# Reordering three queues of a mixture-of-experts stage: later weight pieces behind the tokens' rest, a norm's variance product behind the up products, the last norm's scaling last

## The reference, cut to what matters

```python
x = _layernorm(x + _L0_ffn_ref(x, gate_weight, gate_up_weights, down_weights, shared_gate_up, shared_down))
# in _L0_ffn_ref: 8 routed experts (F = 352), the best two for each token, and one shared expert (Fs = 704)
gu = einsum('th,efh->tef', x, gate_up_weights)
act = silu(gu[..., :F]) * gu[..., F:]
y = einsum('tef,te,ehf->th', act, combine, down_weights)
sgu = x @ shared_gate_up.T
y = y + (silu(sgu[:, :Fs]) * sgu[:, Fs:]) @ shared_down.T
```

## Time and profile before

| | us |
|---|---|
| median of 3 runs | 2788.96 |
| lowest and highest run | 2785.35, 2795.74 |
| the profiled execution's own time | 2776.36 |
| its span, first to last instruction | 2774.6 |
| routed experts, TensorE's first to last product | about 863 to 1142 |
| shared experts, second part | about 1142 to 1292 |
| scan and last sublayer | 1292 to 2774.6 |

### The profile page before, as it was taken

One profiled execution on the slowest core, in us unless ns is written; L12 is line 12 of the kernel. 1 busy time (PEld: TensorE's weight loads), 2 busy tenths in 40 slices (PEclk: granted clock), 3 DMA queues, 4 the chain that ended last, 5 costly groups with the idle time before them and its releaser, 6 DMA issues.

```text
span 2774.6 us, 33259 instructions
## 1 busy us (share of the span) xinstructions
PE 2510.3 (90%) x11786; PEld 1464.5 (53%) x11786; DVE 1854.8 (67%) x2240; ACT 1258.9 (45%) x1997; POOL 1384.6 (50%) x741
## 2 busy tenths in 40 slices
PE   7999939999999999989578899989989888999998
PEld 2555614444677888865233333333333333677776
DVE  5678865554665666555689889889978888722223
ACT  4434105531234666433556655764665442334333
POOL 0222339960050000330499999999999996222221
PEclk9989769989999999999799999999999999999999
DMA  6443863432064777531375786677577555000000
GB/s 225 140 122 103 97 110 89 96 99 92 12 240 158 259 261 259 185 111 52 96 195 150 183 214 175 172 198 218 163 200 213 172 193 206 30 1 16 16 1 31
DMA packets 278967, 384.98 MB, mean 139 GB/s; under 512 B 127104, under 2 KB 148608, under 8 KB 271392
## 3 DMA queue, kind: packets, MB, share of 16 engines
q1 hardware_dynamic: 268944, 335.77, 41.5%
q0 software_dynamic: 9296, 38.80, 5.7%
q10 hardware_dynamic: 576, 8.39, 0.7%
HBM read 312.91 MB, written 59.51 MB: 134 GB/s over the span
## 4 chain that ended last, share of the span: by engine, by line
PE 56%; POOL 15%; DVE 12%; issue 6%; SPq 5%; ACT 4%; DMA 3%; PEldq 0%; DVEq 0%; ACTq 0%; POOLq 0%; PEld 0%
POOL arena L786 8%; PE psum L2036 8%; POOL arena L792 5%; PE psum L1983 4%; PE psum L2217 4%; PE psum L2218 4%; PE psum L2835 4%; SPq L2295 4%; PE psum L3024 2%; PE psum L2190 2%; PE psum L2191 2%; PE psum L2824 2%; PE psum L483 2%; PE psum L1879 1%; DVE psum L1566 1%
## 5 line engine op out<-in xcount | busy, mean ns | idle before, releaser
L786 POOL TENSOR_TENSOR arena<-arena 128x1024 f32<-128x1024 f32 x256 | 626.9, 2468 | 132.9 <-DVE arena L1551 82.8
L2036 PE MATMUL psum<-arena,cst 128*128 128x512 f32 x1024 | 508.2, 632 | 103.6 <-POOL arena L792 92.7
L1090 ACT ACTIVATE psum<-arena,negA 128x512 f32<-128x512 f32 x512 | 333.4, 682 | 322.9 <-DVE arena L1566 280.8
L2036 PEld LDWEIGHTS psum<-arena,cst 128*128 128x128 f32 x1024 | 189.7, 197 | 403.2 <-issue 216.2
L1566 DVE TENSOR_TENSOR_SCAN arena<-psum,arena 128x512 f32<-128x512 f32 x256 | 310.5, 1213 | 57.7 <-ACT psum L1090 37.1
L1566 DVE TENSOR_TENSOR_SCAN psum<-psum,arena 128x512 f32<-128x512 f32 x256 | 298.6, 1212 | 60.9 <-POOL arena L786 56.6
L792 POOL TENSOR_TENSOR arena<-arena 128x1024 f32<-128x1024 f32 x128 | 312.9, 2445 | 2.9 <-DVE arena L1566 2.9
L840 POOL TENSOR_TENSOR arena<-arena 128x512 f32<-128x512 f32 x64 | 92.3, 1442 | 324.0 <-ACT arena L1214 298.9
L1983 PE MATMUL psum<-arena 128*128 128x512 f32 x512 | 231.3, 595 | 1.3 <-PE psum L1983 0.8
L2371 POOL TENSOR_TENSOR arena<-arena,cst 128x1024 f32<-128x1024 f32 x96 | 185.2, 1958 | 42.1 <-PE psum L2938 24.9
L2383 POOL TENSOR_TENSOR arena<-arena,cst 128x512 f32<-128x512 f32 x64 | 76.3, 1218 | 259.4 <-DVE arena L2687 166.4
(11 more groups left out here) (373 smaller groups left out, 4992.6 us busy)
## 6 DMA issues: line engine op xcount, KB each, us to landing
arena<-bc_scr SPq DMA_DIRECT2D x256, 512.0 KB, 5.5
arena<-w_exp SPq DMA_DIRECT2D x23, 1408.0 KB, 6.1
arena<-in_gu SPq DMA_DIRECT2D x48, 512.0 KB, 5.1
arena<-in_inw SPq DMA_DIRECT2D x32, 512.0 KB, 4.3
arena<-in_dn SPq DMA_DIRECT2D x31, 512.0 KB, 6.9
x_scr<-arena SPq DMA_DIRECT2D x19, 512.0 KB, 5.9
arena<-in_x SPq DMA_DIRECT2D x8, 1024.0 KB, 9.8
w_exp<-in_gu SPq DMA_DIRECT2D x16, 512.0 KB, 7.2
```

The source lines that it names most:

```text
L786: nc.gpsimd.tensor_tensor(dB[:, k % 4], du[:, j:j + 2], BC[:, k % RING, 0].unsqueeze(1).broadcast_to([P, 2, T]), ALU.mult).then_inc(s["db_ ...
L1090: nc.scalar.activation(psum[:, bank], dt[:, b % 2, j + t], ACT.Exp, scale=negA2[:, at:at + 1]).then_inc(s["da_ok"], 1)
L2036: ins = mm(psum[:, t], ident, dB[:, k % 4, t], start=False, stop=(n == NS - 1), skip_group_check=True)
```

## The change

- ScalarE, routed: `hi` of the pieces is cut in three: ahead of `silu_b`, behind `act_hi`, behind `tokens_hi`. Against before, only the fourth half of each five differs: there, piece (2, 2) goes from ahead of `silu_b` to behind `act_hi` and piece (2, 3) from there to behind `tokens_hi`. In half 37 piece (22, 3) goes ahead of `silu_b`.
- VectorE, routed: in the first, second and third half of each five the last piece goes from ahead of `act_b` to behind `tokens_lo`; in the fourth half two pieces do, one of them from ahead of `act_lo`. The fifth half keeps its order, since the gate products right behind it need both pieces.
- TensorE, shared: in steps 18, 20 and 22 the variance product (`var_pe`) goes behind the up products.
- VectorE, shared: the last of the three `scale_dve` goes from the end of step 22 to behind step 23, ahead of `add_shared(B - 1)`.

```diff
@@ ScalarE, routed experts
             for h in range(NH):
-                if h:
-                    for k, j in pieces(h)[:-1]:
-                        hi(k, j)
+                first, then = pieces(h)
+                for k, j in first:
+                    hi(k, j)
                 silu_b(h)
                 if h:
                     act_hi(h - 1)
-                    for k, j in pieces(h)[-1:]:
+                    for k, j in then[:1]:
                         hi(k, j)
                 if h == NH - 1:
                     round_x(2)
                 if h + 1 < NH:
                     tokens_hi(h + 1)
-                if h == 0:
-                    for k, j in pieces(h):
-                        hi(k, j)
+                for k, j in then[1 if h else 0:]:
+                    hi(k, j)
@@ VectorE, routed experts
             for h in range(NH):
+                first, then = pieces(h)
+                for k, j in first:
+                    lo(k, j)
                 if h:
-                    for k, j in pieces(h)[:-1]:
-                        lo(k, j)
                     act_lo(h - 1)
-                    for k, j in pieces(h)[-1:]:
+                if h % 5 == 4:
+                    for k, j in then:
                         lo(k, j)
                 act_b(h)
                 if h + 1 < NH:
                     tokens_lo(h + 1)
-                if h == 0:
-                    for k, j in pieces(h):
+                if h % 5 != 4:
+                    for k, j in then:
                         lo(k, j)
@@ VectorE, shared experts, steps 12 to 23
-                if part == 1:
+                if part == 1 and n < NS2 - 2:
                     scale_dve(dve, B + b)
                 if n == NA + 3:
                     rest_x(3)
+            scale_dve(dve, 2 * B - 2)
             add_shared(B - 1)
@@ the plan of the pieces
+        EARLY = (2, 1, 1, 1, 1)
         def pieces(h):
             at = [(3 * (h // 5) + k, j) for k, j in PIECE_AT[h % 5]]
-            return [(k, j) for k, j in at if 0 < k < NBLK]
+            cut = EARLY[h % 5] if h else 0
+            return [[(k, j) for k, j in part if 0 < k < NBLK] for part in (at[:cut], at[cut:])]
@@ TensorE, shared experts, steps 12 to 23
+                gate_or_up(n, 1)
                 if part == 1:
                     var_pe(pe, B + b)
-                gate_or_up(n, 1)
```

## The result

| | us |
|---|---|
| before, median of 8 runs | 2790.01 (2777.27 to 2795.74) |
| changed, median of 8 runs | 2761.9 (2754.09 to 2770.3) |
| ratio, 95% interval | 0.9906, 0.9889 to 0.9923 |
| predicted | 2764, range 2753 to 2779 |
| changed kernel's profiled execution, own time and span | 2761.05, 2759.2 |

The account below looks back on a forecast made before the run. The prediction took TensorE as the bound, holding 56% of the chain. Its terms, 9.3 + 9.5 + 6.4 - 0.3 = 24.9 us, taken as 25 off the median 2788.96, gave 2764 us, range 2753 to 2779.

Parts of the forecast that it names:

- Routed experts: Routed stretch: moving pieces removes TensorE waits for the rest of tokens and activations; 9.3 us saved, bounds 7 to 12.
- a price of 0.40 and 0.5 for a wait: Routed stretch: a removed wait ahead of gate products saves 0.40 us, the one ahead of down products 0.5.
- The weight loads: Routed third block of each group: reload lands about 0.7 us late, spare time covers it; nothing taken, bound 2.4 us.
- Variance products: Shared steps 18, 20, 22: up products fill the 3.46 us wait, saving 9.5 us, plus 6.4 from TensorE's clock.
- The clock's share: Shared variance products: with the shorter wait TensorE's clock stays up; 6.4 us saved, bounds 0 and 6.4.
- the term for the rest: Shared variance products without the clock: 3.18 us of up products moved into the wait in three places, 9.5 us.
- The last scaling: End of the shared stretch: moving the scaling behind step 23 costs 0.3 us, between a 0.1 gain and a 2 loss.
- the 5.6 us now stand ahead of `add_shared`: End of the shared stretch: reciprocal and product delay `add_shared` from 1291.72 to 1292.1, and the scan's first projection waits.
- the clock did not fall at the variance products: Answers the rival that the clock still falls at the shared variance products: 18.5 us saved, 2770.5, chance 0.12.
- The new wait in place of the routed ones: Rival, routed stretch: late weights' cast or `act_lo` behind another piece makes a new wait; 15.6 us saved, 2773, chance 0.12.
- the late reload: Rival, routed stretch: the third block's reload lands so late that every group stalls; slower than before, chance 0.05.
- The rest of the kernel: Rival: the first two rivals together, or other stretches give some gain back; about 9 us saved, 2780, chance 0.12.

Follow-up runs that it names:

- e1: The kernel before with only the routed piece order changed, on ScalarE and VectorE: 2781.48 against 2790.57 us, ratio 0.9965.
- e8: The changed kernel without GpSimd's sums of the two experts' rows, only their semaphore raised: 2760.27 us, ratio 0.9890 to the kernel before.
- e9: The changed kernel with one more, unused reciprocal on VectorE ahead of the last scaling: 2763.41 against 2779.92 us for the kernel before, ratio 0.9937.
- e10: The changed kernel with the last residual sum (`add_shared`) ahead of the last scaling instead of behind it: 2766.67 us, ratio 0.9949 to the kernel before.
- e11: The changed kernel with 12 more small products ahead of the first routed down products: 2757.8 against 2779.92 us for the kernel before, ratio 0.9920.
- e3: The kernel before with only the last scaling moved behind step 23: 2790.62 against 2790.57 us, ratio 0.9996.
- e7: The changed kernel with the fourth half of each five back in its old order on both engines: 2770.82 us, ratio 0.9918 to the kernel before.
- e4: The kernel before with the up products of steps 18, 20 and 22 also made once ahead of the variance product: 2784.03 against 2790.57 us, ratio 0.9970.

## Why the prediction was right

The predicted 2764 stands against 2761.9, and 24.9 us against 26 (21 to 31). Step by step:

- **Routed experts, 9.3 us.** The order of waits was as counted: those ahead of the second and fourth half and that of the down products went, one stayed, five halves took 33.84 us (33.8 predicted, a price of 0.40 and 0.5 for a wait). The stretch alone is 5.6 us shorter in the two profiles, because the execution of before was the one in four without a fall of the clock behind the first weights, which cost 2.7 us. Four profiles of the old order have 279.5, 280.5, 282.0 and 281.4 us, six of the new (the changed kernel twice, e1, e8, e9, e10) 272.3 to 273.8, mean 272.9: 7.9 us, with late weight loads in each of the six.
- **The weight loads.** The step said that the third block's reload would land 0.7 us too late and that the spare time just covers it, with up to 0.4 us in each group as the bound. In the changed kernel's profile four casts of that kind waited, 0.15 to 1.73 us. Only the longest was felt: that group took 34.56 us, 0.7 more. The same group, the second, was the longest in most runs of the new order. So the loads cost about 0.2 to 0.7 us in all, 1.3 in e11, where the prediction took nothing and a bound of 2.4.
- **Variance products, 9.5 + 6.4 us.** The three steps gained 14.7 us, of 15.9. Wait and clock went as said; the term for the rest was 1.2 us too large, since the transposes follow 3.54 us behind the variance product's start where I took the 3.1 that fp32 products followed by an up product take. The clock's share alone was 6.25 us against the profile of before, and would have been 5.1 or 4.6 against those of e1 and e3: the prediction's 6.4 rests on one execution. The low stretch of the clock did not come back behind waits of 0.58 to 0.75 us, in any of the three places of the nine kernels with the new order. By the Trainium skill ("TensorE: Matmul & The Clock Gate", HAM oscillation — how this bites in real kernels) waits between bursts take the clock down; the trace agrees at 3.2 to 3.5 us, where it fell in most executions and not in all.
- **What I left out.** 1.1 us went in steps 19 to 21, where VectorE's instructions met GpSimd's sums. The moved work changed when they meet; in two of the three profiles with TensorE's old order (e1, e3) a meeting cost more than that.
- **The last scaling, a loss of 0.3 us: wrong.** It is a gain of 1.8. The step that failed is "the 5.6 us now stand ahead of `add_shared`", so that the scan waits for VectorE's queue to pass this point. The semaphore is raised as soon as the waits ahead of it are over, while the scaling still runs. The reciprocal ended at 1279.1, about when the down products did, so TensorE was held by its own work and stood 0.52 us there, where the prediction looked for over 2.
- The shared stretch came out at 15.5 us less, 15.6 predicted, but by errors that cancel: -1.2, -1.1 and +2.1. And it is a difference of two executions: the old order took 149.4, 157.2 (e1) and 150.8 us (e3, with the scaling moved), the new one 133.8 to 134.0 in four profiles and 139.8 in a fifth (e7). That the total of 24.9 meets the measured 26 so closely is luck in part.

The rivals: the clock did not fall at the variance products in any profile of the new order. The new wait in place of the routed ones and the late reload are seen in part, as casts that wait for a weight load, at the 0.2 to 1.3 us above. The rest of the kernel did not give the gain back.

## What to carry to other kernels

Where an engine works through a queue by hand, put in the middle of it first what another engine waits for and last what is only needed a step later, and count the price of each wait in distances between starts, not in the idle time: 0.56 us of idle cost 0.40. Work that can fill a long wait of TensorE can be worth more than the wait, because the clock comes with it: 2.8 us a place for the wait here, and 1.5 to 2.1 for the clock. And a semaphore that stands behind instructions in a queue need not wait for their work: look for the last wait ahead of it.

## What the runs showed of the hardware

- A raise of a semaphore by VectorE's queue (`sem_inc`, no instruction of the engine) took effect 0.24 to 0.5 us behind the start of an instruction that had just passed its own wait (L472: 1279.12 to 1279.61, 1286.83 to 1287.17, 1286.20 to 1286.44; 0.66 in e7), in the first two with a residual sum of 2.28 us still queued ahead of it.
- A subtraction on VectorE with both inputs in SBUF (L1380) takes 0.69 us, but 1.79 us (3.28 in e1, 3.29 in e3) while GpSimd adds two SBUF tiles (L764), and the scaling 3.22 instead of 2.29; GpSimd's two sums took 3.46 instead of 2.5 us. Without the sums no such instruction is long. The Trainium skill ("SBUF — State Buffer", Who interferes with whom) says that such an instruction of VectorE and one of GpSimd that reads SBUF hold a read interface in turn, the later one blocked until the first ends; the trace agrees, with 1.1 us for one meeting and 2.6 in e1 and e3.
- Behind the same wait of 3.1 to 3.3 us TensorE's clock fell from 2.4 to 1.2 GHz in ten of twelve kernels' profiles; with 12 small products in the wait (1.25 us left) it stayed at 2.4 in the one profile taken. Behind the waits of 3.45 to 3.47 us ahead of the variance products it fell in all nine places (before, e1, e3); with 12 up products in the wait (0.75 us left, e4) in none of three.
